# Who writes the normalised token tile: one VectorE instruction, or a 128x1 VectorE shift and one ScalarE activation

## What is computed

```
def _layernorm(x, axis=-1, eps=1e-05):
    m = jnp.mean(x, axis=axis, keepdims=True)
    v = jnp.var(x, axis=axis, keepdims=True)
    return (x - m) / jnp.sqrt(v + eps)
x = x + _L0_xattn_ref(_layernorm(x), ctx, ...)   # 32 heads, RMS-normed q and k
x = x + _L0_ffn_ref(_layernorm(x), ...)          # binary weights, routed scales
x = x + _L1_xattn_ref(_layernorm(x), ctx, ...)   # one wide head
x = x + _L1_ffn_ref(_layernorm(x), ...)          # linear with a Fourier-coded update
x = x + _L2_xattn_ref(_layernorm(x), ctx, ...)   # 32 heads, mask and position bias
x = x + _L2_ffn_ref(_layernorm(x), ...)
x = x + _L3_xattn_ref(_layernorm(x), ctx, ...)
x = x + _L3_ffn_ref(_layernorm(x), ...)
```

## Time and profile before

| what | value |
|---|---|
| time, median of three runs | 2228.72 us |
| time of the profiled execution | 2227.87 us |
| its span | 2226.0 us |
| mean granted TensorE clock | 0.976 |
| PE busy | 2070.7 us (93%) |
| DVE busy | 1346.4 us (60%) |
| ACT busy | 1177.3 us (53%) |
| POOL busy | 556.5 us (25%) |

### The profile page before, as it was taken

The page is one execution under the profiler, slowest core; times in us unless marked ns, Lnnn a source line. Parts: engine busy times, 40 slices in busy tenths (PEclk is TensorE's granted clock), DMA queues, the critical chain, the costliest instruction groups (busy, mean ns, idle before and its releaser), DMA issues.

```text
span 2226.0 us, 40366 instructions
## 1 busy us (share of the span) xinstructions
PE 2070.7 (93%) x13732; PEld 1132.2 (51%) x13732; DVE 1346.4 (60%) x2722; ACT 1177.3 (53%) x3031; POOL 556.5 (25%) x958
## 2 busy tenths in 40 slices
PE   6899999999888899999999999998889899999998
PEld 3556565565544445554555455555334455555564
DVE  6567676676664846665666566646542466666664
ACT  6666666676432345554555455533222566666651
POOL 4233232332341412221222122212200222222221
PEclk9899999999998899999999999999979999999999
DMA  3221121221103113232232232111200233333211
GB/s 129 60 65 58 47 63 40 65 61 53 29 1 127 60 50 93 74 93 68 74 93 74 68 88 78 49 36 44 111 19 1 60 79 76 78 78 75 62 49 38
DMA packets 181333, 142.88 MB, mean 64 GB/s; under 512 B 158138, under 2 KB 166586, under 8 KB 171282
## 3 DMA queue, kind: packets, MB, share of 16 engines
q1 hardware_dynamic: 180690, 140.37, 22.4%
q10 hardware_dynamic: 448, 0.03, 0.0%
HBM read 100.26 MB, written 2.10 MB: 46 GB/s over the span
## 4 chain that ended last, share of the span: by engine, by line
PE 62%; DVE 15%; ACT 12%; issue 7%; POOL 2%; DMA 1%; DVEq 0%; ACTq 0%; POOLq 0%; SPq 0%
PE bank L85 19%; PE bank L86 18%; PE bank L87 18%; ACT m_E L558 3%; PE bank L2117 3%; DVE m_Sm L993 2%; ACT m_arena L426 2%; ACT m_arena L537 2%; DVE m_x L1044 2%; DVE m_A L1038 1%; DVE m_nmax L1010 1%; ACT m_arena L528 1%; ACT m_arena L529 1%; DVE m_arena L939 1%; DVE m_arena L838 1%
## 5 line engine op out<-in xcount | busy, mean ns | idle before, releaser
L939 DVE TENSOR_TENSOR m_arena<-bank,m_arena 128x512 f16<-128x512 f32 x320 | 221.4, 692 | 479.2 <-ACT m_arena L537 478.9
L85 PE MATMUL bank<-m_input_parts,m_arena 128*128 128x512 f16 x1120 | 431.8, 386 | 21.9 <-issue 5.7
L86 PE MATMUL bank<-m_input_parts,m_arena 128*128 128x512 f16 x1120 | 431.2, 385 | 0.0
L87 PE MATMUL bank<-m_input_parts,m_arena 128*128 128x512 f16 x1120 | 430.2, 384 | 0.0
L1056 POOL TENSOR_TENSOR m_E<-m_E,m_rinv 128x512 f32<-128x512 f32 (+1 forms) x192 | 172.5, 899 | 805.4 <-DVE m_rinv L1024 805.4
L558 ACT ACTIVATE m_E<-m_Sm,m_nmax 128x64 f32<-128x64 f32 (+1 forms) x512 | 185.4, 363 | 285.1 <-DVE m_nmax L1014 149.0
L537 ACT ACTIVATE m_arena<-bank 128x512 f16<-128x512 f32 x320 | 189.4, 592 | 241.9 <-PE bank L87 241.6
L86 PE MATMUL bank<-m_wo_t,m_A 128*128 128x512 f16 x768 | 293.1, 382 | 0.0
L85 PE MATMUL bank<-m_wo_t,m_A 128*128 128x512 f16 x768 | 293.0, 382 | 0.0
L87 PE MATMUL bank<-m_wo_t,m_A 128*128 128x512 f16 x768 | 292.7, 381 | 0.0
L85 PE MATMUL bank<-m_arena,m_input_parts 128*128 128x128 f16 (+1 forms) x768 | 186.7, 274 | 7.5 <-DVE m_arena L944 6.7
(11 more groups left out here) (308 smaller groups left out, 4163.2 us busy)
## 6 DMA issues: line engine op xcount, KB each, us to landing
m_raw<-a_q SPq DMA_DIRECT2D x24, 1024.0 KB, 5.0
m_raw<-a_o SPq DMA_DIRECT2D x24, 1024.0 KB, 4.9
m_raw<-a_k SPq DMA_DIRECT2D x9, 1024.0 KB, 4.8
m_raw<-a_v SPq DMA_DIRECT2D x9, 1024.0 KB, 5.0
m_bias_in<-bias SPq DMA_DIRECT2D x64, 128.0 KB, 2.1
m_arena<-f_w SPq DMA_DIRECT2D x3, 1024.0 KB, 7.7
m_PT<-m_split SPq DMA_TRANSPOSE x174, 3.0
m_x<-x SPq DMA_DIRECT2D x2, 1024.0 KB, 7.1
```

The costliest lines, as they stand in the source:

```text
L85: pe.matmul(out, lhs[0], rhs[0], start=first, stop=False)
L86: pe.matmul(out, lhs[0], rhs[1], start=False, stop=False)
L87: return pe.matmul(out, lhs[1], rhs[0], start=False, stop=last)
L939: ins = dve.tensor_tensor(self.dest(name, part, 1), self.shaped(name, bank[m % 2][:, :]), self.dest(name, part, 0), ALU.subtract)
```

## The change

In x1, f1 and a2 DVE no longer makes the normalised tile. It makes `shift = -mean * rstd`, 128x1, and ACT makes `Identity(x * rstd + shift)` over 128x512. The waits for the double buffer move with it to ACT. The other five norms stay on DVE. ACT's new instruction stands first in `act_step`, ahead of the copy of the turned tile. In `BinaryFFN.act` the follower's steps start one step earlier, so that tile 0 has its norm. `shift` becomes a 128x8 tile with a semaphore of its own in each of the three blocks.

```diff
@@ class Attention (used where layer == 2, a2)
     def act_step(self, act, t):
 
+        if self.layer == 2 and 1 <= t <= TILES:
+            self.norm_act(act, t - 1)
         if 2 <= t:
             self.turn_high(act, t - 2)
...
+    def shift(self, dve, t):
+        k, s = self.k, self.s
+        dve.tensor_scalar(k.shift[:, t:t + 1], k.mv[:, t, 0:1], k.rstd[:, t:t + 1], -1.0, ALU.mult,
+                          ALU.mult).then_inc(s["shift"].sem, 1)
+
+    def norm_act(self, act, t):
+        k, s = self.k, self.s
+        act.wait_ge(*s["shift"].by(t + 1))
+        act.wait_ge(*s["xt"].by(t - 1))
+        act.activation(k.Sm[:, t % 2, :], k.x[:, t, :], ACT.Identity, bias=k.shift[:, t:t + 1],
+                       scale=k.rstd[:, t:t + 1]).then_inc(s["xn"].sem, 1)
...
             dve.wait_ge(*self.s["rstd"].by(t))
-            self.norm(dve, t - 1)
+            (self.shift if self.layer == 2 else self.norm)(dve, t - 1)
@@ class Front (x1 and f1; shift and norm_act as above, on self.xn, shift also waits for rstd)
         if t < TILES:
             self.stat(dve, t)
         if 1 <= t <= TILES:
-            self.norm(dve, t - 1)
+            self.shift(dve, t - 1)
...
     def act_step(self, act, t):
+        if 1 <= t <= TILES:
+            self.norm_act(act, t - 1)
         if 2 <= t:
             self.keep_turned(act, t - 2)
@@ BinaryFFN.act
-            if i >= 4:
+            if i >= 3:
                 self.next.act_step(act, i - 2)
```

More of the change, by code:

```diff
@@ L121, in __init__ @@
         names += {0: ["k_tot", "k_rs", "k_n", "k_nhi", "k_nlo", "q_tot", "q_rs"],
-                  2: ["bias0", "bias1", "bias_sum", "masks"],
+                  2: ["shift", "bias0", "bias1", "bias_sum", "masks"],
                   3: ["kv", "kv_hi", "kv_lo", "ctx_in", "ctx_hi", "ctx_lo", "kv_scale"]}[layer]
@@ L131, in __init__ @@
         totals |= dict.fromkeys(("proj", "proj_hi", "proj_lo"), 16 * self.NT)
-        totals |= dict.fromkeys(("xn", "xt", "xt_hi", "xt_lo"), TILES)
+        totals |= dict.fromkeys(("shift", "xn", "xt", "xt_hi", "xt_lo"), TILES)
         totals |= dict.fromkeys(("scores", "top", "exped", "rinv", "probs", "split_hi", "split_lo",
@@ L1195, in __init__ @@
         self.turns = 2
-        totals = {"stat": TILES, "rstd": TILES, "xn": TILES, "xt": TILES, "xt_s": TILES, "x": TILES, "xb": TILES}
+        totals = {"stat": TILES, "rstd": TILES, "xn": TILES, "xt": TILES, "xt_s": TILES, "x": TILES, "xb": TILES, "shift": TILES}
         for n in own:
@@ L1216, in norm, with shift, norm_act @@
                           ALU.subtract, ALU.mult).then_inc(s["xn"].sem, 1)
+    def shift(self, dve, t):
+        k, s = self.k, self.s
+        dve.wait_ge(*s["rstd"].by(t + 1))
+        dve.tensor_scalar(k.shift[:, t:t + 1], k.mv[:, t, 0:1], k.rstd[:, t:t + 1], -1.0, ALU.mult,
+                          ALU.mult).then_inc(s["shift"].sem, 1)
+    def norm_act(self, act, t):
+        k, s = self.k, self.s
+        act.wait_ge(*s["shift"].by(t + 1))
+        act.wait_ge(*s["xt"].by(t - 1))
+        act.activation(self.xn[:, t % 2, :], k.x[:, t, :], ACT.Identity, bias=k.shift[:, t:t + 1],
+                       scale=k.rstd[:, t:t + 1]).then_inc(s["xn"].sem, 1)
     def turn(self, pe, t):
@@ L1629, in __init__ @@
     def __init__(self, k, ffn, dram):
-        super().__init__(k, "x1", ["xt_hi", "proj", "proj_s", "scores", "top", "ex", "rinv", "probs",
+        super().__init__(k, "x1", ["xt_hi", "shift", "proj", "proj_s", "scores", "top", "ex", "rinv", "probs",
                                    "turned", "pt", "mixed"], ffn.s["x"], 1, dram)
@@ L1804, in __init__ @@
     def __init__(self, k, x1, dram):
-        super().__init__(k, "f1", ["masked", "ws", "g", "g_s", "delta", "merged", "xb", "main"], x1.s["x"], 1, dram,
-                         ("stat", "rstd", "xn", "xt", "x"))
+        super().__init__(k, "f1", ["shift", "ws", "g", "g_s", "delta", "merged", "xb", "main"], x1.s["x"], 1, dram,
+                         ("stat", "rstd", "xn", "xt", "x", "shift"))
         v = k.view
@@ L2430, in __init__ @@
         self.bn, self.mv = sb("bn", [P, TILES, 6]), sb("mv", [P, TILES, 2])
-        self.var, self.rstd = for_all("var", 8), for_all("rstd", 8)
+        self.var, self.rstd, self.shift = for_all("var", 8), for_all("rstd", 8), for_all("shift", 8)
         self.bank = [ctx.enter_context(nc.psum_tensor(f"bank{i}", [P, 512], FP32)) for i in range(8)]
```

## The result

The changed kernel takes **2240.5 us** (median of 5 runs, 2237.8 to 2243.4). The kernel before took 2228.7 beside it (5 runs). The ratio is 1.005, with a 95% interval of 1.0038 to 1.0062, so the change costs 8.5 to 13.8 us. Forecast were 2242 us, in a range of 2233 to 2251, and "slower". The profiled execution of the changed kernel took 2237.8 us with a span of 2236.0.

The account below looks back on a forecast made before the run. DVE was taken to bound both loops, ACT's room depending on order. Terms 7.9 + 6.3 + 10.0 - 4.9 - 3.1 - 2.3 = +13.9 us on 2227.87 gave 2241.8, stated as 2242 for the median; range 2233 to 2251.

Parts of the forecast that it names:

- First loop: Loop at 646 to 676 us: DVE is the chain, so six norms taken off it count 0.38 each; -2.3 us.
- T: Second loop, DVE's wait before the slab's sum, three times: 2.97 us each, against 1.01 once before; +7.9 us.
- L: Second loop, DVE's wait before the slab's low half: 2.72 us for q and k, 1.2 for v; +6.3 us.
- K: Second loop, DVE's wait before a2's own low half, eight times: 1.43 us each; +10.0 us.
- Relief: Second loop: 13 norms leave DVE where it rules, -4.9 us; DVE no longer meeting POOL adds -3.1 us.
- The meeting with POOL: Second loop: DVE's instructions no longer run longer beside POOL's `add_bias`; -3.1 us, ends 0 and 5.0.
- The relief alone: Rival, both loops: ACT's room is usable, so DVE's chain only shortens, by 10.3 us, to 2217.6; 8%.
- K alone: Rival, second loop: slab work stays hidden, only a2's low halves wait; -0.3 us, 2227.6, no change; 9%.
- TensorE's clock: Rival, second loop: PE idles before k's and v's slab sums, then runs main products at half clock; +6.9 us, 2248.7; 13%.

Follow-up runs that it names:

- f1 alone: The kernel before with only f1's eight norms moved to ACT, x1's and a2's left on DVE: 2240.6 us, ratio 1.0051.
- x1 alone: The kernel before with only x1's eight norms moved to ACT, f1's and a2's left on DVE: 2227.2 us, ratio 0.999.
- the slab work first: The changed kernel with ACT doing, in each second-loop step, the slab's squares or f16 copy, then f1's copy and norm, then a2's: 2227.5 us, ratio 0.9998.
- the new instruction twice: The changed kernel with ACT's new activation issued twice in f1 and a2, the first into scratch: 2253.7 us, ratio 1.0112 to the kernel before.
- the copy first: The changed kernel with ACT's copy of the turned tile ahead of the new norm in f1 and a2: 2236.0 us, 1.0038 to the kernel before.

## Why the prediction was right

**What bounds.** DVE in both loops: right. That the busy shares of the earlier trace rows say nothing of ACT's room at the right moment was the argument that decided, and f1 alone against x1 alone shows it.

**The durations.** The new activation was taken at 0.78 us with 0.68 of ACT's time, and measured 0.81 with 0.72 (736.59 to 737.31). The formula of the Trainium skill ("ScalarE: Activation LUTs", "What ACT_TABLE_LOAD costs") gave an estimate of 0.80, closer than the neighbouring row. The shift was taken at 0.15 with 0.08 held, and measured 0.20 with 0.12 (736.35 to 736.47): it reads `rstd` as a second 128x1 operand where L1223 has a constant, which the row chosen could not show. It also does two operations and L1223 one, but other rows of the kernel before put the time down to the operand: over 128x4 and with one operation each, L981 with such an operand takes 0.23 us and L1014 with a constant 0.17. A tile thus gives DVE 0.34 us back and not 0.38. The copies took 0.57 and not 0.60, holding 0.48.

**First loop.** Forecast −2.3, measured −2.1; six norms at 0.34 are 2.04. x1 alone shows it apart from the rest, with a second loop that is unchanged to 0.1 us. One link was not foreseen: where PE leaves the loop it no longer waits for DVE's low half, as in the earlier trace rows, but for ACT's norm:

```profile
671.76 0.66 PE L1250 MATMUL bank<-m_ident,m_Sm 128*128 128x128 f32 x4 [0.86 <-ACT m_Sm L1242]
```

**T, L, K.** The idle time in a row runs from the end of the instruction before, while DVE's next one can start 0.08 us ahead of that end; so a wait costs 0.08 more than its row says. From start to start, less what DVE's own instructions hold, T is 733.54 − 729.76 − 0.12 − 0.60 = 3.06 (forecast 2.97), L is 739.80 − 736.35 − 0.72 = 2.73 (2.72), for v 771.39 − 769.62 − 0.60 = 1.17 (1.2), and K is 751.35 − 749.78 − 0.12 = 1.45 (1.43). With before's waits taken the same way (1.09, 0.38 and 1.30) that makes 9.2 − 1.1 = **+8.1** for +7.9; 2 × 2.73 + 1.17 − 0.38 = **+6.2** for +6.3; and seven K with a last one of 0.72, 10.15 + 0.72 − 1.30 = **+9.6** for +10.0, since the last wait shrank a little.

**Relief.** 13 × 0.34 = 4.4 and not 4.9, the one term that was off by as much as 0.5. The meeting with POOL is gone as forecast, L840 at its undisturbed length three times (group by line, 640 to 790 us; the other row is the new activation):

```profile
L840 DVE SCALAR_TENSOR_TENSOR m_arena<-m_raw,m_w_scale,m_arena 128x2048 f16<-128x2048 f32 x3 | 7.1, 2351 | 6.4 <-ACT m_arena L431 6.4
L1242 ACT ACTIVATE m_arena<-m_x,m_shift,m_rstd 128x512 f32<-128x512 f32 x8 | 6.5, 813 | 22.3 <-DVE m_shift L1235 22.3
```

**Sum.** With measured terms: 8.1 + 6.2 + 9.6 − 4.4 − 3.1 = +16.4 for the second loop, which grew by 16.1; forecast were 16.2. That forecast and measurement meet within 0.1 us is in part luck, since K was 0.4 too high and the relief 0.5. a2's f16 projections start at 788.28, near the 788 forecast. Both loops give +14.0, the forecast sum was +13.9, and the medians give +11.8 (8.5 to 13.8 by the interval). (The last step of the forecast was also rounded down: 2241.8 and 0.85 are 2242.6, and it says 2242.) The two profiled spans differ by only 10.0. The difference to 14.0 lies outside the loops, in code that is the same: +0.7 ahead of them, −1.0 between them and −3.8 behind. From the last low half to the end of the span it took 1452.3 us before and 1448.5 with the change, and in two executions of the kernel with the slab work first 1448.4 and 1451.9; between the loops these two took 19.2 and 21.0. A single profile can't resolve 2 us of this span, and whether the medians' 2 us are more than chance is open.

**The rivals.** *The relief alone* fell with the three waits, *K alone* with T and L. *TensorE's clock* is the instructive one. The clock did fall, to 0.87 and 0.71 in the second loop; PE was idle 5.33 and 6.15 us before the sums of k and v, about the 5.7 forecast, and ran the next instructions at half speed:

```profile
748.50 0.16 PE L633 MATMUL bank<-m_w_ss,m_ones_b 128*128 128x1 bf16 x1 [5.33 <-ACT m_arena L426]
748.62 1.09 PE L644 MATMUL bank<-m_ident,m_Sm 128*128 128x128 f32 x4
749.50 1.92 PE L1819 MATMUL bank<-m_arena,m_E 128*128 128x512 f32 x2
...
768.02 4.20 PE L1909 MATMUL bank<-m_arena 128*128 128x512 f32 x8
...
785.75 1.12 PE L644 MATMUL bank<-m_ident,m_Sm 128*128 128x128 f32 x4 [1.06 <-ACT m_Sm L865]
```

x1's product took 1.92 us instead of 1.02 (L1819 at 738.27). f1's main products, which the rival priced at twice their time, took 3.65 and 4.20 instead of 3.60, since the clock was back at 0.98 from 752 to 756. And after step 4 DVE waited for neither in the changed kernel (L1773 and L1930 follow without idling). The first half of the rival's condition held and the second didn't. What the clock may have cost is the last turn, 1.12 us instead of 0.60: ACT's copy waits for it and DVE for the copy (0.63), so at most 0.5 us, and the last turns ran at half clock in the kernel before too. With the new instruction twice, with the copy first and with f1 alone DVE did wait for an x1 product once each, by 0.84, 0.39 and 0.39 us: the rival was close to mattering, though by another product than the one it named (L1901's).

## What to carry to other kernels

Before moving work between engines in a kernel whose order is written out, write down what stands behind it in the receiving engine's stream, and when its input is ready: an instruction that waits late makes all that is behind it late, however idle the engine. Place such an instruction last in its step, behind everything whose inputs are there already; here that was worth 13 us, against 0.26 us a tile for the slower engine. Even so the move only broke even here (ratio 0.9998 to the kernel before). And cost each swap by following the next dependency too: waits of one chain don't subtract one by one, as the copy put first showed (5.2 us of the 12 that the hand sum struck out).

## What the runs showed of the hardware

A second 128x1 operand in place of a constant cost a `tensor_scalar` on DVE 0.05 us in length (0.20 for 0.15) and 0.04 us of the engine's time. The slab's 128x2048 `scalar_tensor_tensor` takes 2.35 us alone and longer beside POOL's addition of 1.26 us, by nearly all of the time that both run: in the kernel before the three ran 1.11, 1.13 and 0.55 us beside it and took 0.91, 0.93 and 0.35 us more. With the slab work first two of the three met it again, for 1.24 and 1.23 us, and took 1.03 more each. TensorE's granted clock differed between two executions of the same kernel, 0.79 and 1.00 in the same stretch.
